# Clearing the masked triangle on GpSimd instead of adding a mask on TensorE, in a decoder layer on one core

## The reference

```
scores = jnp.einsum('bsnh,btnh->bnst', k, q) / math.sqrt(HEAD_SIZE)
scores = jnp.triu(scores) + -10000.0 * jnp.tril(ones, k=-1)
attn = jax.nn.softmax(scores, axis=2)
out = jnp.einsum('bnkq,bknh->bqnh', attn, v)
...
return out @ Wo + bo
```

## Time and profile before

| | us |
|---|---|
| median of 3 runs | 1549.02 (1548.85 to 1554.98) |
| the profiled execution | 1547.28 |
| its span in the trace | 1545.5 |
| first pass | about 8 to 159 |
| three middle passes | about 159 to 668 |
| last pass and experts | 668 to 1545 |

### The profile page before, as it was taken

The page is one execution under the profiler, slowest core; times in us unless marked ns, Lnnn a source line. Parts: engine busy times, 40 slices in busy tenths (PEclk is TensorE's granted clock), DMA queues, the critical chain, the costliest instruction groups (busy, mean ns, idle before and its releaser), DMA issues.

```text
span 1545.5 us, 24712 instructions
## 1 busy us (share of the span) xinstructions
PE 1388.1 (90%) x7587; PEld 1020.6 (66%) x7595; DVE 908.7 (59%) x1574; ACT 418.3 (27%) x628; POOL 341.8 (22%) x294
## 2 busy tenths in 40 slices
PE   7998998999998999957987999899999999887992
PEld 3454454444554445436776888799999999786891
DVE  2442787568865886678664787533443344656534
ACT  1132132402332133321112011222332233434423
POOL 3000000000100010031000284243443344343432
PEclk9979998899979998978998999999999999998996
DMA  8521433215212522320410101544654455859447
GB/s 266 140 74 41 148 83 99 70 56 164 69 45 68 180 80 69 132 70 14 140 61 22 42 28 35 162 84 81 139 128 82 82 135 132 234 125 271 78 82 241
DMA packets 90127, 164.28 MB, mean 106 GB/s; under 512 B 8544, under 2 KB 29536, under 8 KB 89968
## 3 DMA queue, kind: packets, MB, share of 16 engines
q1 hardware_dynamic: 73168, 122.88, 25.5%
q0 software_dynamic: 16816, 39.59, 13.8%
HBM read 113.42 MB, written 49.02 MB: 105 GB/s over the span
## 4 chain that ended last, share of the span: by engine, by line
PE 47%; issue 36%; DVE 7%; DMA 5%; POOL 2%; ACT 1%; SPq 1%; DVEq 1%; ACTq 0%; POOLq 0%
PE psUA L1006 12%; PE psUB L1006 11%; PE psY L1013 8%; PE psR L1013 4%; PE psTX L989 2%; PE psR L1098 2%; PE psTH L1022 2%; DMA room<-in_L_ffn_w_dram 2%; POOL xr L800 1%; PE psST L1188 1%; DMA xr<-in_x_dram 1%; DVE x L1478 1%; ACT w_s L860 1%; PE psOT L1207 1%; PE psR L1061 1%
## 5 line engine op out<-in xcount | busy, mean ns | idle before, releaser
L1006 PE MATMUL psUA<-w_s,xgT 128*128 (+1 forms) x1284 | 246.3, 342 | 2.1 <-DVE xgT L1384 1.8
L1006 PE MATMUL psUB<-w_s,xgT 128*128 (+1 forms) x1284 | 225.0, 324 | 0.0
L1006 PEld LDWEIGHTS psUA<-w_s,xgT 128*128 128x128 f32 x1284 | 215.5, 197 | 9.8 <-issue 8.0
L1006 PEld LDWEIGHTS psUB<-w_s,xgT 128*128 128x128 f32 x1284 | 211.3, 190 | 0.0
L830 POOL DMA_INDIRECT sx_d<-yg,dst_i x74 | 119.5, 1615 | 302.2 <-ACT yg L909 261.3
L869 ACT ACTIVATE silg<-psUA 128x352 f32<-128x352 f32 x107 | 49.6, 464 | 445.6 <-PE psUB L1006 445.6
L1013 PE MATMUL psY<-w_s,hgT 128*128 (+3 forms) x621 | 161.4, 404 | 0.2 <-issue 0.2
L1572 DVE TENSOR_REDUCE nm<-psR 128x1 f32<-128x128 f32 (+3 forms) x256 | 114.7, 487 | 69.7 <-PE psR L1176 64.6
L1393 DVE SCALAR_TENSOR_TENSOR hg<-silg,cws,psUB 128x352 f32<-128x352 f32 x75 | 43.4, 579 | 175.7 <-ACT silg L869 175.7
L1013 PEld LDWEIGHTS psY<-w_s,hgT 128*128 128x128 f32 (+1 forms) x621 | 113.4, 190 | 22.2 <-issue 0.4
L1098 PE MATMUL psR<-xT,room 128*128 128x512 f32 x256 | 120.2, 617 | 2.4 <-ACT xT L919 2.4
(11 more groups left out here) (225 smaller groups left out, 2103.3 us busy)
## 6 DMA issues: line engine op xcount, KB each, us to landing
room<-in_L_ffn_w_dram SPq DMA_DIRECT2D x32, 704.0 KB, 6.0
scr_d<-qhl SPq DMA_DIRECT2D x32, 512.0 KB, 3.7
qst<-scr_d SPq DMA_DIRECT2D x48, 256.0 KB, 3.9
kst<-scr_d SPq DMA_DIRECT2D x48, 256.0 KB, 5.9
room<-in_L_ffn_w_dram SPq DMA_DIRECT2D x16, 512.0 KB, 7.2
xt<-in_x_dram SPq DMA_DIRECT2D x5, 1024.0 KB, 7.8
xr<-in_x_dram SPq DMA_DIRECT2D x4, 1024.0 KB, 5.4
breg<-in_fside_BxS2xS_dram SPq DMA_DIRECT2D x4, 1024.0 KB, 8.0
```

The lines of the kernel that those rows point to most:

```text
L1006: mm = pe.matmul(t[:, 0:F], xgT[:, par, a_, c * P:(c + 1) * P], w[:, buf, b_, c, :], start=(c == 0 and n == 0), stop=(c == C - 1 and n == ...
```

## The change

GpSimd clears the masked triangle in `pT` after the exponential; the mask products, `mask_kq` and its setup go; `weigh` waits for the new semaphore `s_sel` instead of `s_exp`. The four bias additions go from `rows:1` to the steps `scores:6` to `scores:9`, one each, behind that head's selects. The two `split` steps of the last pass go from GpSimd to DVE, which uses the function it has for the routed experts.

```diff
@@ gpsimd @@
-            fill(mask_kq[:, :], 0.0)
...
-            cut(mask_kq[:, :], [[1, P]], 0, -1, ALU.is_ge, NEG)
...
-                    if x[0] == "split":
-                        split(x[1])
-                    elif x[0] in ("ln1", "ln2"):
+                    if x[0] in ("ln1", "ln2"):
                         power(b, ST, halfn)
                     elif x[0] == "s":
                         power(b, C2 if x[1] else C, halfp)
-                    elif x == ("rows", 1):
-
-                        if b is None:
-                            pool.wait_ge(s_wlast, 48)
-                        pool.wait_ge(s_xr, 16 * (a + 1))
-                        for i in range(ST):
+                    elif x[0] == "scores":
+                        h = x[1]
+                        for m, blocks in enumerate((((0, 1),), ((S, 1), (2 * S - P, 2)))):
+                            pool.wait_ge(s_exp, a * (2 * HEADS) + 2 * h + m + 1)
+                            apart(pool)
+                            for lo, nb_ in blocks:
+                                p_ = pT[:, h % 4, lo:lo + nb_ * P].rearrange("p (n q) -> p n q", n=nb_)
+                                pool.affine_select(out=p_, in_=p_, compare_op=ALU.is_ge, fill=0.0, base=0,
+                                                   pattern=[[0, nb_], [1, P]], channel_multiplier=-1).then_inc(s_sel, 1)
+                        if 6 <= h < 6 + ST:
+                            i = h - 6
+                            if i == 0:
+                                if b is None:
+                                    pool.wait_ge(s_wlast, 48)
+                                pool.wait_ge(s_xr, 16 * (a + 1))
                             pool.tensor_tensor(xr[:, i, :], xr[:, i, :], bo_bc[:, :], ALU.add).then_inc(s_xrb, 1)
@@ tensor, scores @@
-                            pe.matmul(psST[:, o:o + w], kst[0:98, i, j, kb * P:(kb + 1) * P], qst[0:98, i, j, S - w:S],
-                                      start=True, stop=False)
-                            mm = pe.matmul(psST[:, KOFF[kb]:KOFF[kb] + P], identb[:, :], mask_kq[:, :], start=False,
-                                           stop=True)
+                            mm = pe.matmul(psST[:, o:o + w], kst[0:98, i, j, kb * P:(kb + 1) * P], qst[0:98, i, j, S - w:S],
+                                           start=True, stop=True)
@@ tensor, weigh @@
-                        pe.wait_ge(s_exp, a * (2 * HEADS) + 4 * p_ + 3 + part)
+                        pe.wait_ge(s_sel, a * (3 * HEADS) + 6 * p_ + (6 if part else 4))
@@ vector @@
+                    elif kind == "split":
+                        split(n, n, UP + DOWN)
```

More of the change, by code:

```diff
@@ L66, in decoder_layer @@
         mask_qk = sb("mask_qk", [P, P], BF16)
-        mask_kq = sb("mask_kq", [P, P], BF16)
         hot = sb("hot", [P, 4, 32])
@@ L125, in decoder_layer @@
         s_exp = sem("s_exp")
+        s_sel = sem("s_sel")
         s_pv = sem("s_pv")
@@ L730, in _ @@
         def _(pool):
[L731 to L735, removed]
             n = [0]
@@ L1099, in product @@
                 return mm
-            pe.wait_ge(s_const, 16)
+            pe.wait_ge(s_const, 15)
             pe.wait_ge(s_wfirst, 32)
@@ L1442, in _ @@
             dve.wait_ge(s_wfirst, 32)
-            dve.wait_ge(s_const, 16)
+            dve.wait_ge(s_const, 15)
             dve.wait_ge(s_gw, 1)
```

## The result

The changed kernel takes 1493.05 us (median of 4 runs, 1491.09 to 1499.52); the kernel before, on the same chip, 1548.93 (1547.03 to 1554.98). The ratio is 0.9648, 95% interval 0.9624 to 0.9673.

The account below looks back on a forecast made before the run. TensorE was taken to set the pace, busy 90%. Terms 37.6 - 2.9 - 1.3 - 14.4 + 0.3 + 10 + 7.1 = 36.4 us off 1547.28 gave 1510.9, forecast as 1513 for the median; range 1500 to 1536.

Parts of the forecast that it names:

- Masks: Attention scores: removing four mask products saves 0.51 us a head at full clock, 0.92 at half; 37.6 us in all.
- the forecast's own sign: At full clock, a head from first scores product to the next step near 0.66 us; 0.96 for the columns rival.
- the dense places: Where heads and maxima alternate, part of the mask saving is lost: 0.7 us a middle pass, 0.3 in the first.
- The rival of columns alone: Scores: a mask is worth only its 128 columns, 0.053 us, so masks give 16 us; total 1529; chance 0.13.
- The cost of the selects at `ln2`: `weigh:12` waits for selects behind `ln2`'s power; 4.8 us lost in each of three middle passes, 14.4 in all.
- The rival in which DVE and GpSimd alternate: At `ln2`, selects and normalising take turns, `weigh:12` at 293.3, clock falls 17 us: 35 lost, 1533; chance 0.13.
- Bias: Spreading the additions over heads 6 to 9 gains 3.3 us a pass, 10 in three passes.
- the mechanism at `s:1`: GpSimd's one-piece bias addition slows DVE, so TensorE waits 2.13 us, then runs at lower clock; spreading it removes the wait.
- Splits: Last pass: two splits moved to DVE free its normalising and small instructions; 3.5 and 3.6 us gained, 7.1 together.
- The failed step: Before `max:12`: additions delaying DVE's `xq:1` cost nothing, since TensorE waits there for the stack load anyway.
- each pass has such a stretch: Each pass keeps a half-clock stretch with three heads; the other 13 run at full clock.

Follow-up runs that it names:

- bias alone: Kernel before with only the four bias additions moved to heads 6 to 9, masks and splits as before: 1538.05 us, ratio 0.993.
- splits alone: Kernel before with only the last pass's two splits moved from GpSimd to DVE: 1540.63 us, ratio 0.996.
- masks back: Changed kernel with the mask products computed as well, beside the selects: 1529.43 us, ratio 0.989.
- selects alone: Kernel before with GpSimd selects in place of the mask products, bias and splits as before: 1520.93 us, ratio 0.983.
- bias at `rows:1`: Changed kernel with its four bias additions back in one piece at `rows:1`: 1510.89 us, ratio 0.977.
- heads 8 to 11: Changed kernel with the bias additions at heads 8 to 11 instead of 6 to 9: 1497.55 us, then 1501.32 us when run again.
- one at head 6: Changed kernel with the bias additions at heads 6, 8, 9 and 10: 1494.74 us, then 1491.56 us when run again.
- later power: Changed kernel with GpSimd doing `ln2`'s power behind head 13's selects instead of ahead of head 12's: 1482.74 us, ratio 0.960.

## Why the prediction missed

**Masks: right for a head, too high for a pass.** 0.51 us a head was forecast at full clock and 0.92 at half. By the forecast's own sign, from a head's first product to the next step, it is 0.44 and 0.81; with the maxima behind it 0.52 and 0.97. A middle pass can be split up: its length from one `ln2` power to the next, less PE's idles of 0.3 us and more, less 0.45 of its half-clock time (the share lost, 1 - 1.17/2.13 of the earlier trace rows). For the second and third middle pass that leaves 150 us before (170.4 - 9.6 - 0.45 x 24) and 144.4 after (means of 155.9 - 10.0 - 0.45 x 3.4 and 153.8 - 9.6). 5.6 us are saved. As the lost clock is taken out already, all 16 heads count at the full-clock price: 16 x 0.51 - 0.7 = 7.5 was forecast, so the dense places gave back nearly 2 us a pass more than the 0.7 set down for them. The rival of columns alone (0.21 a head) falls. The Trainium skill ("TensorE: Matmul & The Clock Gate", Back-to-back issue gap) gives the formula that led to it for an isolated product; for a stream of weight loads and products of 128 columns it has about 81 ns. The 0.44 to 0.52 us for four masks are 0.11 to 0.13 us each, above both.

**The cost of the selects at `ln2`: right in kind, too high.** I put an idle of 2.8 us and 2.0 us of lowered clock there. The idle is 1.82 (and 0.40 at `weigh:10`), 2.2 in all, and no lowered clock stood behind it in the profiled execution. Taking the wait at `weigh:12` away gives 3.4 to 4.2 us a pass, part of which is clock in other places. The rival in which DVE and GpSimd alternate falls with the 2.00 us of DVE's normalising, and no other run gave it back. The Trainium skill ("SBUF — State Buffer", Who interferes with whom) has the engine that comes second fully blocked, where both use the port pair that they share. The trace agrees for DVE's `xsc`, held for 1.12 us beside an addition of 1.27, and for GpSimd's select, held for 2.23 us beside DVE's addition of 2.29. It shows no such block between the selects and the normalisings at `ln2`, where both went on, though the splits had stretched the same kind of normalising.

**Bias: right in place, and the mechanism at `s:1` worked as described.** 10 us forecast, 10 alone. What stood next was not TensorE itself but the row of maxima, 1.38, 0.98 and 0.69 us.

**Splits: right.** 7.1 forecast, 7.7 by the trace and 7.6 by the medians of that kernel; 7.2 in the changed one.

**The failed step** is the one that set the stack wait at nothing: "In the new place single additions of 1.24 us delay DVE's xq:1, behind which TensorE waits for the stack load anyway: nothing", and with it the assumption in the first part that "each pass has such a stretch". I priced a delay inside a wait by its length. That is right for the idle (it shrank from 8.5 us to 5.5 over four passes) and wrong for the clock behind it. The half-clock time at `max:12` went from 68.4 us to 20.4 in the profiled executions: 48 x 0.45 = 21.6 us. 4.9 of these I had booked already (12 heads at 0.92 instead of 0.51), which leaves 16.7. The profiled executions' gain exceeds the forecast by 1545.5 - 1492.6 - 36.4 = 16.5. That the two agree so well is partly luck, as other misses happen to cancel. Up to the start of the last pass the gain is 49.5 us against 29 forecast, so 20 more. Towards these 20, beside the 16.7, go 3.0 us of idle that the stack wait lost and 7.8 at `ln2` (3 x 2.6); against them go some 5 us in the dense places and 3.0 of waits for the row of maxima. The last pass gained 7.2 as forecast. The experts behind it took 795.0 us instead of 791.2 in this execution; in the other traces, with the same work there, they took 790.0 to 793.3, and why they took more here is not known. The second trace of the changed kernel, with 34.1 us instead of 20.4 at `max:12`, would give 34.3 x 0.45 = 15.4 in place of 21.6.

Two things shortened the stretches. Over the traces, the mean half-clock time behind a **middle** `max:12` is 15.4 us with masks and a whole idle (12 places: before, bias alone, splits alone, masks back), 12.2 without masks and a whole idle (12: selects alone, bias at `rows:1`, heads 8 to 11 twice), and 3.4 without masks and with a cut idle (15: the changed kernel twice, one at head 6 twice, later power; in 7 of them the load had landed before the second stop, and only the first was left). In the first pass, where nothing cuts the idle, it is 17.1 with masks and 11.7 without. The cut is confirmed by time as well, at 5.5 to 6 us. In the two kernels with masks and with additions at heads 6 to 9 the idle stayed whole: with the bias alone although an addition met `xsc` in all three middle passes (0.95 us), with the masks put back because it missed `xsc` in all three. That the cut needs the masks gone is argued from the first of these and not shown by a run of its own. It is the likely source of the 10 us which the parts alone don't show; the stretches that are shorter without masks are in the 27 us of the selects already.

**Open** is why a stretch without masks ends sooner, why two whole idles of 2.00 and 2.15 us had none behind them, and why short stretches stand behind the same wait at `ln2` in some executions and not in others. By the traces, moving the addition away from head 6 adds 22 us at half clock in three passes, 10 us of time; 5.5 to 6 were measured, within what ten runs can tell (give or take 4).

## What to carry to other kernels

Price an idle of the pacing engine by what the granted clock does behind it, not by its length: here 8.5 us of waits cost 43. Before forecasting a change, look for the waits behind which the clock is low and ask of each whether the change lengthens, shortens or cuts it, even when it seems hidden there. And when a change gains more than its parts, take the suspected wait away in both kernels: the distance between them then shows how much of the gain hung on that wait (33 us of 56 here). What is left is not the change's work alone, for the clock can fall behind other waits instead: here 23 us were left, with some 8 us of such clock in the changed kernel, where the work alone was expected to be worth 35.

## What the runs showed of the hardware

- An idle of 1.8 to 3.0 us before `max:12` was followed by 10 to 20 us at 1.2 GHz in 35 of the 37 traced places where it stood whole. The length alone does not decide: the wait of 1.8 us at `ln2` had nothing behind it in 21 of 30 traced places and 3.4 us in the nine others, and one of 3.13 us at the diagonals of `s:1` had nothing behind it in five of nine. In the first trace of the changed kernel the clock stayed at 1.00 behind `ln2` (427 to 445 us):

```profile
427.00:445.00 18.00, 15.59 (x107) 6.74 (x106) 7.83 (x9) 8.12 (x14) 4.73 (x13) 1.00 0.44 146
```

- DVE and GpSimd held each other up in some pairs and not in others. DVE's `xsc` on 128x4 elements took 1.12 us instead of 0.17 beside GpSimd's addition of 1.27, and GpSimd's select of 128x128 took 2.23 us instead of 0.29 beside DVE's addition over 128x2048, 2.29 us. Four normalisings of 128x512 beside nine selects took 2.00 us instead of 1.92, and the selects 3.45 instead of 2.85.
- A select of 128x128 takes 0.29 us undisturbed, one of 128x256 0.42 in the mean. The mean of 0.36 for 128x128 contains the three that were held for 2.23 us.
